# Attention row turn, output projection and second norm one step later in each frame, and the 28 weight chunks dealt out as 3, 3, 3, 3, 3, 3, 5, 5 instead of 3 and 4 in turn

## The reference

```python
def xattn(q, k, v, mask):
    qh, kh, vh = heads(q @ Wq.T + bq), heads(k @ Wk.T + bk), heads(v @ Wv.T + bv)
    score = where(mask, einsum('bhqd,bhkd->bhqk', qh, kh) / 4, -10000.)
    return merge(softmax(score) @ vh) @ Wo.T + bo
def ffn(x):                       # x as [tokens, 256]
    G, I = top_k(sigmoid(x @ Wg), 2)
    y = gelu(x @ W1[e] + b1[e]) @ W2[e] + b2[e]      # per expert e
    return sum of y over the two chosen experts, weighed with G
x = x + tanh(g_xattn) * xattn(layernorm(x), ctx, ctx, mask)
x = x + tanh(g_ffn) * ffn(layernorm(x))
```

## Time and profile before

| | before |
|---|---|
| median of 3 runs | 526.32 us (523.36 to 526.5) |
| profiled execution | 526.01 us |
| its span, first to last instruction | 524.3 us |
| TensorE busy | 428.4 us, 82% |
| VectorE busy | 332.1 us, 63% |
| ScalarE busy | 217.8 us, 42% |
| mean granted clock of TensorE | 0.893 |
| chain that ended last | PE 60%, DVE 23%, DMA 6% |

### The profile page before, as it was taken

One profiled execution on the slowest core, in us unless ns is written; L12 is line 12 of the kernel. 1 busy time (PEld: TensorE's weight loads), 2 busy tenths in 40 slices (PEclk: granted clock), 3 DMA queues, 4 the chain that ended last, 5 costly groups with the idle time before them and its releaser, 6 DMA issues.

```text
span 524.3 us, 11190 instructions
## 1 busy us (share of the span) xinstructions
PE 428.4 (82%) x4040; PEld 326.2 (62%) x4040; DVE 332.1 (63%) x960; ACT 217.8 (42%) x549; POOL 171.4 (33%) x161
## 2 busy tenths in 40 slices
PE   5367767888888879897247999999999999999980
PEld 3234323555455544545226999999999999999970
DVE  5855687687886867668993555545554555555530
ACT  2130553455555654661004445444544454444420
POOL 8622601020112112111003354455445454554231
PEclk9855678899999997995557999999999999999995
DMA  7443332352535434341101133322322233233211
GB/s 208 103 139 105 81 116 67 90 157 90 152 109 145 128 97 131 115 122 41 46 1 53 32 46 50 53 43 43 55 50 44 43 54 52 42 45 51 33 21 20
DMA packets 35146, 40.26 MB, mean 77 GB/s; under 512 B 10431, under 2 KB 29747, under 8 KB 35091
## 3 DMA queue, kind: packets, MB, share of 16 engines
q0 software_dynamic: 12608, 27.48, 23.3%
q1 hardware_dynamic: 19953, 11.17, 7.6%
q10 hardware_dynamic: 2532, 0.89, 0.8%
HBM read 25.87 MB, written 9.50 MB: 67 GB/s over the span
## 4 chain that ended last, share of the span: by engine, by line
PE 60%; DVE 23%; DMA 6%; issue 4%; ACT 3%; POOL 1%; SPq 0%; ACTq 0%; DVEq 0%; POOLq 0%
PE bank L1218 7%; PE bank L1202 6%; PE bank L1204 6%; PE bank L1203 6%; PE bank L1220 6%; PE bank L1219 6%; PE bank L981 4%; DVE rowmax L666 4%; DMA W_stage<-in_L_ffn_W 3%; PE bank L1019 3%; PE bank L1128 3%; PE bank L998 3%; DVE W L729 2%; DVE stats L613 2%; PE bank L1166 2%
## 5 line engine op out<-in xcount | busy, mean ns | idle before, releaser
L1202 PE MATMUL bank<-xh,W 128*128 128x128 f16 x624 | 121.2, 220 | 1.0 <-DVE xl L896 1.0
L1203 PE MATMUL bank<-xl,W 128*128 128x128 f16 x624 | 121.1, 220 | 0.0
L1204 PE MATMUL bank<-xh,W 128*128 128x128 f16 x624 | 121.1, 220 | 0.0
L581 ACT ACTIVATE h<-bank,b1T 128x128 f32<-128x128 f32 x312 | 89.1, 370 | 70.1 <-PE bank L1204 68.2
L414 POOL DMA_INDIRECT out_rows<-y_sb,scatter_tab x39 | 63.8, 1635 | 113.5 <-DVE y_sb L913 107.4
L1218 PE MATMUL bank<-W,hh 128*128 x312 | 85.5, 274 | 0.0
L1220 PE MATMUL bank<-W,hl 128*128 x312 | 85.0, 273 | 0.0
L1219 PE MATMUL bank<-W,hh 128*128 x312 | 85.0, 273 | 0.0
L904 DVE CAST hh<-h 128x512 f16<-128x512 f32 x78 | 33.8, 434 | 75.9 <-ACT h L581 75.9
L666 DVE TENSOR_REDUCE rowmax<-bank 128x2 f32<-128x308 f32 x128 | 57.1, 475 | 26.1 <-PE bank L998 23.9
L525 ACT ACTIVATE probs<-bank 128x512 f32<-128x512 f32 x80 | 47.2, 595 | 47.9 <-PE bank L1076 36.7
(11 more groups left out here) (182 smaller groups left out, 683.7 us busy)
## 6 DMA issues: line engine op xcount, KB each, us to landing
W_stage<-in_L_ffn_W POOLq DMA_DIRECT2D x32, 512.0 KB, 4.1
xn_scratch<-attn SPq DMA_DIRECT2D x8, 256.0 KB, 2.2
qst<-qh SPq DMA_DIRECT2D x60, 32.0 KB, 2.4
X_late<-in_x SPq DMA_DIRECT2D x6, 256.0 KB, 4.9
out_rows<-X_late SPq DMA_DIRECT2D x6, 256.0 KB, 2.5
qst<-ql SPq DMA_DIRECT2D x28, 32.0 KB, 3.0
xg<-xn_scratch,gather_tab POOLq DMA_INDIRECT x39, 3.1
out_rows<-y_sb,scatter_tab POOLq DMA_INDIRECT x39, 3.9
```

Source lines behind the costliest of these rows:

```text
L581: ins = nc.scalar.activation(h32[s % 4][:, m * P:(m + 1) * P], H_BANKS[s % 4][:, m * P:(m + 1) * P], ACT.Gelu_apprx_tanh, scale=1.0 / W_SC ...
L1202: nc.tensor.matmul(dst, wh, xh[t % 3][:, cut], start=(c == 0), stop=False)
L1203: nc.tensor.matmul(dst, wh, xl[t % 3][:, cut], start=False, stop=False)
L1204: ins = nc.tensor.matmul(dst, wl, xh[t % 3][:, cut], start=False, stop=(c == KC - 1))
```

## The change

Two things. First, for unit u-1 the attention turn with its copy goes from step 4 to step 5, the projection, residual and moments from step 5 to 6, the two refinements from 6 to 7, and the third with the norm from 7 to 8. On TensorE the turn of the maxima keeps step 5, and now stands ahead of the projection. Second, the 28 chunks get other steps: 0, 3, 7 in frames 0 to 5, and 0, 2, 4, 6, 8 in frames 6 and 7. Before, even frames had 0, 3, 7 and odd frames 0, 3, 6, 8.

```diff
-        W_SLOTS = {u: ((0, 3, 7), (0, 3, 6, 8))[u % 2] if u < U else () for u in FRAMES}
+        W_SLOTS = {u: (0, 3, 7) if u < U - 2 else (0, 2, 4, 6, 8) if u < U else () for u in FRAMES}
...
-                    if i == 4 and live(u - 1):
+                    if i == 5 and live(u - 1):
                         v = u - 1
                         act.wait_ge(a_filled, a_nth["attnT", v])
...
-                    if i == 5 and live(u - 1):
+                    if i == 6 and live(u - 1):
                         v = u - 1
                         dve.wait_ge(q_filled, q_nth["wo", v])
...
-                    if i == 6 and live(u - 1):
+                    if i == 7 and live(u - 1):
                         refine_rstd(2, var, rstd, newton)
-                    if i == 7 and live(u - 1):
+                    if i == 8 and live(u - 1):
                         v = u - 1
                         refine_rstd(1, var, rstd, newton)
...
-                    if i == 4 and live(u - 1):
+                    if i == 5 and live(u - 1):
                         v = u - 1
                         a_use("attnT", v)
...
-                    if i == 5 and live(u - 1):
+                    if i == 5 and live(u + 1):
+                        turn_maxima(u + 1)
+                    if i == 6 and live(u - 1):
                         v = u - 1
                         q_use("wo", v)
...
-                    if i == 5 and live(u + 1):
-                        turn_maxima(u + 1)
```

## The result

| | before | after |
|---|---|---|
| median of 4 runs each | 525.46 us (523.36 to 526.5) | 540.76 us (539.93 to 541.19) |
| profiled execution, its span | 526.01, 524.3 us | 539.93, 538.1 us |
| frame 1, 2, 3, 4, 5 | 25.9, 22.3, 23.1, 22.0, 24.5 | 22.4, 23.8, 23.8, 23.9, 23.9 |
| frame 6, 7 (to the tail's first turn) | 17.1, 15.3 | 21.0, 23.5 |
| tail's first turn to the end | 288.8 | 290.5 |

A frame is counted from its first exp to the next one's. The changed kernel takes 1.027 of the time before (95% interval 1.0225 to 1.0315), 15.3 us more by the medians; the predicted time was 534.7 us, and the measured one lies 0.24 us inside the upper end of the range (541).

What follows compares the result with a forecast made beforehand. A ring of hand-overs between engines bounds the frames, and the weights' path frames 6 and 7. Frames 1 to 5 give -0.35, frames 6 and 7 +9.0: +8.65 on 526.01 makes 534.7 us, range 526 to 541.

Steps and rivals of the forecast that it cites:

- The first wait filled, the second born, the residual later: Frames 1 to 5: under 0.4 us before the attention turn, 0.6 to 0.9 before the turned maxima, residual 1.4 late.
- VectorE's wait before the residual: Sign in the profile after: VectorE stands 2 us or more before the residual; in frame 2 before, 1.85.
- VectorE's term, +0.65 a frame: Frames 1 to 5: later residual, less two reduces done ahead of it, lengthens a frame by 0.5 to 0.7 us.
- The three-chunk frames: Three chunks instead of four save 0.8 us each in frames 1 and 3, and 1.35 in frame 5.
- rival D: Frames 6 and 7: less dense TensorE work lowers the clock to 1.2 GHz, +4 to +6 us, 539 to 541; chance 0.15.
- frame 3 as long as frame 2: Sign in the profile after: frames 2 and 3 equally long, both 22.5 to 23.5 us.
- Frames 6 and 7, +9.0: Five chunks each over two buffers: waits for 4.3 us loads move the tail's first turn from 235.5 to 244.5.
- The tail and the experts "as they are": Tail and 39 expert tiles hold the same work in the same order, so they move with length unchanged.
- A: Shift and lighter frames give 9.2 us, chunks cost only their rounds, 4.8: 522 us, faster; chance 0.10.
- B: Shift and lighter frames give 9.2 us, but frames 6 and 7 cost the full 9.0: 526, no change; chance 0.20.
- C: SP's query copies start 1.6 us later, slack falls from 3.7 to about 1; 1 us lost in four frames, 538.5; chance 0.10.
- The ring: Hand-overs that set the frame: weighing, turn, projection, residual, moments and reduces, next frame's maxima, weighing; no engine always busy.

Runs made afterwards that it cites:

- e4: Changed kernel with step 0's four late score matmuls issued five times in frames 2 to 6, filling TensorE's stand: 533.32 us, 1.0151 of before.
- e6: Changed kernel with the refinements and second norm back at steps 6 and 7: 535.08 us, 1.0169 of before.
- e2: Kernel before with only the new chunk steps, turn, projection and norm at their old steps: 537.24 us, 1.0242 of before.
- e8: Kernel before with the new chunk steps and a third staging buffer from frame 6 on: 526.17 us, 1.0008 of before.
- e1: Changed kernel with the chunks of before, so the step shift alone: 536.5 us, 1.0209 of before.
- e5: Step shift with the chunks of before, projection moved ahead of turned maxima and late values: 527.47 us, 1.0032 of before.
- e10: e5 with step 0's late scores issued five times in frames 2 to 6 and frame 5's step 8 scores seven times: 522.75 us, 0.9952 of before.
- e11: e10 with ten matmuls of 512 columns into an unused bank ahead of the first expert tile: 523.41 us, 0.9959 of before.
- e12: e10 with the refinements and second norm back at steps 6 and 7: 523.46 us, 0.9969 of before.
- e7: Changed kernel with both a third staging buffer from frame 6 and repeated score matmuls at the starts of frames 2 to 6: 531.72 us, 1.0109 of before.
- e3: Changed kernel with a third staging buffer from the first chunk of frame 6 on: 537.98 us, 1.0238 of before.

## Why the prediction was right in kind and 6 us short

**The first wait filled, the second born, the residual later: right.** 0.31 us before the attention turn (under 0.4 was forecast), 0.69 before the turned maxima (0.6 to 0.9). From the turn's start the projection begins 2.8 us later (3.0 forecast), and from the residual to the four reduces it is 8.41 us (8.57 forecast, 9.44 before).

One of the signs named in advance came otherwise: VectorE's wait before the residual is 1.25 us, not 2 or more. The reduces that moved ahead of it have waits of their own (0.36 and 0.52 in frame 2), 2.1 us in all.

**VectorE's term, +0.65 a frame: too large.** From the end of weighing to the residual it is 4.87 us (3.7 before, 5.05 forecast), so the reduces stand 0.2 later, not 0.65. At full clock a frame of the shifted kernel is 22.2 (e4, e6), of the unshifted one 22.0 (e2, e8).

**The three-chunk frames: right in sign, its size open.** -2.95 for frames 1 to 5 was forecast; on top of the shift it was -3.1 (117.8 against e1's 120.9). With the chunks alone it was -5.5, because before had 3.4 us of half clock in frame 1 and 6.1 in frame 5, of which only 2.5 are left.

**The clock in frames 2 to 5: the step that failed.** The prediction looked for the half clock in frames 6 and 7 only (rival D), and read TensorE's earlier arrival at the frame's end as harmless ("and then stands before the next frame's first max scores"). That stand of 1.93 us, with the half clock behind it, is what costs 1.6 us in each of the frames, as e4 and e6 show. The term for the shift was 4 x 0.65 = 2.6 in the sum and is 5.5 with the new chunks (117.8 - 112.3); with the chunks of before it is 3.1 (120.9 - 117.8, e1). The two parts don't add, so neither split is the right one. In the first the shift's term is 2.9 us too small and the chunks' gain 2.6 too small, and the errors cancel; in the second both come out near the forecast, with e1's half clock in it. Either way frames 1 to 5 come to 0.0 instead of -0.35, and that is luck: a sum that foresaw no new half clock in these frames met a kernel that has 13.6 us at half level there, where before had 9.5. The forecast of "frame 3 as long as frame 2" held (23.8 both), its 22.5 to 23.5 not.

**Frames 6 and 7, +9.0: the mechanism right, 3.1 short.** The loads took what the rows said (4.4 us in these frames by the list of DMA issues), and ScalarE waited for them at a2, b0 and b2 as replayed (4.8 us), with four more waits 8.3 us in all (6 or more forecast). The Trainium skill's fit in "DMA: Bandwidth & Descriptors", section "Anatomy of one DMA - SWDGE (gpsimd) path", gives an estimate of 3.2 us for such a load; the trace, with 4.4, does not agree with it here. In after: a2's high half 213.09 instead of 211.9, because low a0 starts 1.1 us later, behind a frame start with another 1.15 us stand; from there to the residual 6.9 instead of 5.4 us, because the late values and the projection ran at 1.2 GHz (2.90 us, 1.89 at full clock in frame 2). Those 2.7 us are handed on whole: b0 at 229.75 (226.8 forecast), b2's high half ends at 237.9 (234.8), the residual at 241.34 (238.4), the norm, and the turn at 247.67 (244.5). The rounds of frame 7 themselves were right within 0.2 us. So frames 6 and 7 took 21.0 and 23.5 us, not near 19 and 21, and the tail's first turn came 12.2 us later, not 8 to 9.

**The tail and the experts "as they are": nearly.** Its first part, the last line of the first view, takes 18.7 instead of 17.3 us, with about the same granted clock (0.59 and 0.57), and why is open; the expert tiles took the same 246.5 and 246.9 us. The parts make up the miss: 0.35 in frames 1 to 5, 3.1 in frames 6 and 7 and 1.7 behind them are the 5.2 us by which the profiled execution lies above 534.7, and the median is 0.8 above that one. That the time is inside the range at all, by 0.24 us, is luck as well: its upper end was set for a half clock in frames 6 and 7 alone.

**The rivals.** A (the shift pays in full) falls: e1 is 2.1% slower. B falls with it. C (the query's copies late) did not happen in the changed kernel, whose traces have no wait for them; it showed at 1.6 us in two waits as soon as the projection came early, and in e10 with a half-clock stretch behind the longest (its price of 1 us in four frames gives 538.7, not the 538.5 of the text). D happened, 3.4 us in frame 6 and 4.7 in frame 7, beside frames 2 to 5, where it wasn't looked for. In frames 6 and 7 it shows on the path with about the 1.5 us named above, not with 4 to 6.

The ring itself was read rightly: with the projection early and the clock up, a frame does take 20.8 to 21.0 us (e5, e10, e11, e12), about 1 us under the 22.0 of before. But in no run did all frames keep it: those with four chunks take 22.2 and 22.8 even at full clock (e10), and elsewhere a half-clock stretch takes the gain back (e11 kept it in frames 2 and 4 and had a stretch in frame 1).

**What stays open.** Why frame 2 of e1 and of e6 fell to half clock behind stands of only 0.79 and 0.70 us, why the 2.17 us of frame 1 are followed by it in five profiles of fourteen, and what holds frame 7 of the changed kernel at 22.3 us when no load is waited for any more and frames 2 to 6 are filled (e7). TensorE still stands 2.25 us for the norm there, which the filling doesn't reach; moving the norm back was worth 0.5 us in frame 7 of e6 and 1.1 in that of e12, the remainder was not tried.

## What to carry to other kernels

When an edit makes TensorE arrive earlier at a hand-over that another engine sets, nothing is gained, and the longer stand can bring the clock down for the work behind it: look at the granted clock of each frame, not of the span. A dealing-out of loads over two buffers is bounded by its rounds (low half, issue, landing, high half) and by the places of the halves in the queues, so pack a frame no tighter than that, or add a buffer; and where two waits hide behind each other, as load and norm do here, taking one away shows only part of its price. Repeating a cheap matmul with the same result in a stand is a quick way to find out what the clock costs; look at the frames around it too, since the half clock came up elsewhere in e4 (frame 1) and e7 (frame 5).

## What the runs showed of the hardware

In the frames the half clock came in stretches of 3.4, 6.8, 10.2 or 13.7 us. In the changed kernel one came at the start of each of frames 2 to 5, 0.2 to 0.4 us behind the end of TensorE's 1.93 us stand, in frames in which the engine was busy 20.3 of 23.8 us. At the starts of frames 2 to 5 in all runs of the table every stand of 1.92 us or more (four in the changed kernel, four in e3, two each in e1 and e5) had a half-level stretch behind it; of the stands of 1.2 us or less only the two named above had one. That is no rule for other places: the 2.17 us of frame 1 had none in nine profiles of fourteen, and in frame 2 of e5 and e10 a stand of 1.30 or 1.34 us was enough.

The Trainium skill says of a kernel with short stands between groups of matmuls that work through PSUM banks in turn (TensorE: Matmul & The Clock Gate, section "A second HAM failure mode: psum-queue depth-cycling") that they are frequent enough for the clock to oscillate and that the cost is paid between the bursts. The traces here agree in that the clock of the changed kernel swings between its two levels (1.2 and 2.4 GHz) in frames 2 to 5 with no stand above 1.93 us; here it is one longer stand a frame, and the cost is in the matmuls behind it, 1.6 us for each 3.4 us stretch at the starts of frames 2 to 5 of the changed kernel. And more matmuls made the kernel faster: 16 added in each of five frames gave 7.4 us.
